# Issuing the stores of a two-layer transformer sandwich from ScalarE's DMA queue instead of SyncE's

## What is computed

```python
x = x + _layernorm(_L0_attn_ref(_layernorm(x), mask, weight, bias))
x = x + _layernorm(_L0_ffn_ref(_layernorm(x), W_up, gate_w, expert_bias, lora_A, lora_B))
```

## Time and profile before

| | us |
|---|---|
| median of 2 runs | 1674.51 |
| lowest, highest of them | 1667.52, 1681.50 |
| profiled execution | 1665.05 |
| its span, slowest cores (0 and 7) | 1663.5 |
| its span, fastest core (4) | 1653.5 |

### The profile page before, as it was taken

The page is one execution under the profiler, slowest core; times in us unless marked ns, Lnnn a source line. Parts: engine busy times, 40 slices in busy tenths (PEclk is TensorE's granted clock), DMA queues, the critical chain, the costliest instruction groups (busy, mean ns, idle before and its releaser), DMA issues.

```text
span 1663.5 us, 26761 instructions; the slowest of 8 cores (1653.5 to 1663.5 us)
## 1 busy us (share of the span) xinstructions
PE 1113.3 (67%) x9240; PEld 869.2 (52%) x9240; DVE 573.2 (34%) x805; ACT 393.0 (24%) x1249; POOL 44.6 (3%) x88
## 2 busy tenths in 40 slices
PE   0211369889898999988122132999999999999300
PEld 0100147667676777767011011777777777777200
DVE  1466553654656546444544434000000000001533
ACT  1422432212121222222232332222222222222100
POOL 1000000000000000000000000000000000000000
PEclk9999999999999999999555555999999999999755
DMA  8913235676867677641342762142342343241288
GB/s 194 337 58 102 51 102 133 172 183 173 202 160 196 163 188 198 163 83 52 119 185 101 210 195 101 27 77 52 71 83 52 55 77 74 52 77 27 107 332 319
DMA packets 40000, 220.47 MB, mean 133 GB/s; under 512 B 4850, under 2 KB 4866, under 8 KB 21442
## 3 DMA queue, kind: packets, MB, share of 16 engines
q0 software_dynamic: 11792, 84.46, 25.9%
q1 hardware_dynamic: 27938, 134.30, 23.0%
q10 hardware_dynamic: 144, 0.00, 0.0%
HBM read 252.86 MB, written 33.55 MB: 172 GB/s over the span
## 4 chain that ended last, share of the span: by engine, by line
PE 50%; DVE 20%; DMA 17%; issue 9%; ACT 2%; DVEq 1%; SPq 0%; ACTq 0%; POOL 0%; POOLq 0%
PE pm L375 42%; DMA mring<-mw 12%; PE pt L215 5%; DVE psj_i L304 3%; DVE wmb L347 2%; DMA fm<-xmid 2%; PE pm L389 2%; DVE xbst L271 1%; DVE sums_h L256 1%; DMA mo<-x 1%; DVE mo L539 1%; DVEq L680 1%; DVE cmp L563 1%; DVE fm L658 1%; ACT junk L525 1%
## 5 line engine op out<-in xcount | busy, mean ns | idle before, releaser
L375 PE MATMUL pm<-wmb,fm 128*128 128x256 bf16 x8192 | 952.4, 275 | 38.3 <-PE pt L583 0.2
L375 PEld LDWEIGHTS pm<-wmb,fm 128*128 128x128 bf16 x8192 | 791.3, 99 | 176.7 <-issue 79.9
L395 ACT ACTIVATE mo<-pm 128x256 bf16<-128x256 f32 x256 | 98.3, 384 | 780.2 <-PE pm L382 406.4
L304 DVE TENSOR_REDUCE psj_i<-mring 128x32 int32<-128x1024 int32 x128 | 156.1, 1220 | 217.4 <-DMA mring<-mw 211.0
L215 PE MATMUL pt<-identb,xbst 128*128 128x128 bf16 x288 | 51.4, 288 | 204.5 <-DVE xbst L271 170.8
L186 DVE TENSOR_REDUCE st_d<-acc_s 128x1 f32<-128x16 f32 x8 | 1.4, 170 | 489.5 <-ACT junk L403 488.8
L347 DVE TENSOR_TENSOR wmb<-wmb,bmpj 128x4096 bf16<-128x4096 bf16 x32 | 141.6, 4425 | 11.7 <-DMA wmb<-bw 8.5
L215 PEld LDWEIGHTS pt<-identb,xbst 128*128 128x128 bf16 x288 | 24.8, 115 | 231.1 <-issue 231.1
L215 PE MATMUL pt<-identb,mo 128*128 128x128 bf16 x224 | 39.7, 288 | 102.1 <-DVE mo L539 93.7
L403 ACT ACTIVATE junk<-pm 128x256 bf16<-128x256 f32 x256 | 98.3, 384 | 23.8 <-ACT mo L395 0.4
L220 ACT COPY fm<-pt 128x512 bf16<-128x512 bf16 x128 | 75.0, 586 | 115.1 <-PE pt L215 115.1
(11 more groups left out here) (116 smaller groups left out, 364.5 us busy)
## 6 DMA issues: line engine op xcount, KB each, us to landing
mring<-mw SPq DMA_DIRECT2D x128, 512.0 KB, 5.2
wmb<-bw POOLq DMA_DIRECT2D x32, 1024.0 KB, 9.8
wmb<-bu POOLq DMA_DIRECT2D x32, 1024.0 KB, 7.9
mo<-x POOLq DMA_DIRECT2D x12, 1024.0 KB, 25.9
xst<-x SPq DMA_DIRECT2D x10, 1024.0 KB, 8.4
xmid<-xst SPq DMA_DIRECT2D x10, 1024.0 KB, 4.6
fm<-xmid SPq DMA_DIRECT2D x8, 1024.0 KB, 8.2
y<-fm SPq DMA_DIRECT2D x8, 1024.0 KB, 4.5
```

The lines of the kernel that those rows point to most:

```text
L304: return e.tensor_reduce(out=psj_i32[:, (j % 2) * 256 + pc * 32:(j % 2) * 256 + (pc + 1) * 32], in_=mring[idx % 2][:, :].rearrange("p (g w ...
L375: return e.matmul(bank[0:128, 0:NS], fm[:, k * 1024 + i * 128:k * 1024 + i * 128 + 128], wmb[j % 2][:, k * NS:(k + 1) * NS], start=(k == 0 ...
L395: return e.activation(out=mo[:, i * 4096 + j * NS:i * 4096 + (j + 1) * NS], in_=bank[0:128, 0:NS], func=AF.Identity, accum_out=acc_s[:, i ...
```

## The change

The engine that issues two kinds of stores is ScalarE instead of SyncE: the 16 stores to `xmid` in the middle stage and the 16 stores to `y` in the tail. Waits, semaphores, sizes and slots are as before. All loads stay on SyncE.

```diff
@@ -519,7 +519,7 @@
                         scalar=c_one[:, 0:1], in1=ap_slot,
                         op0=ALU.mult, op1=ALU.add, accum_out=sums_h[:, sl:sl + 1])
                 trh[h] = E("vector", fr, waits=[td[h], t_tmp, t_const], inc="sV")
-                xm_tok[(i, h)] = E("sync", lambda e, i=i, h=h, ap_slot=slots[h][0]: e.dma_start(
+                xm_tok[(i, h)] = E("scalar", lambda e, i=i, h=h, ap_slot=slots[h][0]: e.dma_start(
                     out=d_xmid[i * 128:(i + 1) * 128, h * HALF:(h + 1) * HALF], in_=ap_slot),
                     waits=[trh[h]], inc=store_sem(), amt=16)
                 tq = E("scalar", lambda e, ap_slot=slots[h][0], sl=sl: e.activation(
@@ -658,7 +658,7 @@
                 tos[h] = E("vector", lambda e, i=i, h=h, ap_slot=slots[h][0]: e.tensor_add(
                     ap_slot, ap_slot, mo[:, i * 4096 + h * HALF:i * 4096 + (h + 1) * HALF]),
                     waits=[td[h], t_tmp], inc="sV")
-                y_tok[(i, h)] = E("sync", lambda e, i=i, h=h, ap_slot=slots[h][0]: e.dma_start(
+                y_tok[(i, h)] = E("scalar", lambda e, i=i, h=h, ap_slot=slots[h][0]: e.dma_start(
                     out=o_y[i * 128:(i + 1) * 128, h * HALF:(h + 1) * HALF], in_=ap_slot),
                     waits=[tos[h]], inc=store_sem(), amt=16)
```

## The result

| | before | after |
|---|---|---|
| median of the runs, us | 1673.64 (10 runs) | 1651.90 (11 runs) |
| lowest, us | 1667.27 | 1648.02 |
| profiled execution, us | 1665.05 | 1651.42 |
| span of its slowest core | 1663.5 (0 and 7) | 1649.9 (5) |

The changed kernel takes 0.987 of the time before (95% interval 0.984 to 0.990, over the runs in the undisturbed state): 1.3% or some 22 us less, under 2%. The forecast was 1637 with a range of 1624 to 1658. The sign and the mechanism hold. The sum of the forecast was 28.9 us less; the medians differ by 21.7 and the profiled executions by 13.6.

The account below looks back on a forecast made before the run. The prediction took SyncE's list order, which keeps the tail's loads behind stores, as the bound. From the profiled 1665.05 us, less 32.9 in the tail, plus 4.0 in the middle stage, it got 1636.2, said 1637, range 1624 to 1658.

Parts of the forecast that it names:

- What bounds the kernel now: Tail: list order on SyncE keeps loads behind stores, a serial round of about 13 us a chunk, eight rounds.
- Tail, instruction side: Tail: load 1 issued during matmuls, loads 2 to 5 at 1552.8, adds done early, DMA engines the next bound.
- Tail, the term of the rate: Tail: 29.4 MB at 385 GB/s take 76.3 us, gain 32.9 us; bounds 326 and 424 GB/s.
- Middle stage: Middle stage: stores ahead of squares on ScalarE make square 1 0.5 us late; cost 4.0 us over eight chunks, 2.6 to 6.6.
- Sum: Whole kernel: profiled execution 1665.05 less 32.9 in the tail plus 4.0 in the middle stage, 1636.2 us.
- the two queues share badly: Tail: turns between loads and stores keep 326 to 360 GB/s, gain 19 to 27, time 1642 to 1650 us; chance 0.20.
- The queues share well: Tail: engines carry 405 to 424 GB/s, gain 37 to 40 us, time 1629 to 1632; chance 0.20.
- The tail doesn't move: Tail: DMA engines already the bound, so reordering issues does nothing; time 1669 us; chance 0.06.
- the slower case: Middle stage: each store issue holds ScalarE until its transfer lands, costing 70 us, time 1702; chance 0.04.

Follow-up runs that it names:

- sp_order: Against the kernel before: all DMAs stay on SyncE, only its list's order in the tail changes, loads of chunks 0 to 5 first; ratio 0.988, tail 87.9 to 93.0 us.

## Why the prediction came out as it did

**What bounds the kernel now.** Right. The lists kept the loads back, and the waits of the earlier trace rows are gone. `sp_order` shows that a new order alone, in one queue, is enough.

**Tail, instruction side.** Right at each point: load 1 while TensorE works, loads 2 to 5 at the last matmul, a share near 1 to the end, last add 20 us ahead of the end, DMA the new bound.

**Tail, the term of the rate.** This is the term that was mis-sized. I took 385 GB/s, "between 375 and 424 and nearer the first", for a gain of 32.9 us. Measured on core 5: 29.4 MB in 89.0 - 1.5 us, 336 GB/s, a gain of 22 to 23. At the forecast's own lower bound of 326 the sum gave 19.1, so the size is one that the bounds held but the choice missed. I read the rate from stretches of 4 to 8 us of a tail in which the neighbour had gaps, and took it for what the core would get when neither has any. My ground for that, 424 and 420 on cores 7 and 6 in the same window, was weak on two counts: 4 us are too short to say what lasts, and windows count from each core's own first instruction, which no row shows to be the same moment. A longer row was there, 345 GB/s at a share of 1.00 over 10 us at the entry; it shows one core, and I used it only for a rival. The same trace has it for all: from 40 to 80 us the eight cores move 334 to 344 GB/s each at a share of 0.99 to 1.00. With 345 the sum reads 29.4 / 0.345 = 85.1, plus 1.5, end at 1639.4, gain 24.1, and 1665.05 - 24.1 + 4.0 = 1645. Most of the gain needs no higher rate at all: at the old mean of 326 it would be 19.1 by the forecast's own sum. It comes from the 15.8 us after the last matmul (1552.8 to 1568.6) in which the core moved only 61 GB/s and now streams.

The Trainium skill (HBM Reference, Specifications (TRN2)) gives about 358 GB/s for each core of a pair when both stream and more for a core alone. The runs agree with it in kind: 336 to 347 in the mix on eight cores, 427 to 428 alone. I had set it against the trace and held the trace to disagree; it was my reading of the trace that was wrong, not the rule.

**Middle stage.** The mechanism was right to the instruction: one issue shows ahead of square 0, and store 1 must wait for square 0 and then delays square 1. The size was 4.0 us, measured 5.6 (0.70 a chunk), within 2.6 to 6.6. What was missing is small waits. In chunk 1 square 1 starts 0.72 us behind its add's end, 0.58 more than before, near the 0.5 taken. But chunk 1, from which the price was read, is the cheapest: the waits at L169 grew by 0.56 us there, and by 0.95 or more in chunks 2 and 5, where square 0 too came some 0.3 us later behind its store.

**Sum.** 22 to 23 less 5.6 is 17; the profiled executions differ by 13.6, because the slowest core entered the middle stage 2.0 us later and lost 0.7 in the projection, and the runs' medians by 21.7. The difference between these is the spread of the runs. It also moves the forecast: 1637 starts from an execution of 1665.05, and the median before is 1673.64, 8.6 above it. The tail's rate (some 10), the middle stage (1.6) and the low start (8.6) add up to 20 us; the median missed 1637 by only 15. The other 5 us are the spread of the runs, which is luck.

**The rivals.** Of mine, "the two queues share badly" gives the right rate (326 to 360) and tail gain (19 to 27), a time that misses by 2 us (1642 to 1650), and the wrong cause: `sp_order` has one queue and the same rate, and the single core has two queues and 428. "The queues share well" is what one core alone does. "The tail doesn't move" was out, and with it the reading of the Trainium skill's rule on spreading DMAs over engines as one that forbids a gain (DMA: Bandwidth & Descriptors, Rules for kernel authors): no bandwidth was gained, only order. ScalarE was not held by its issues in the middle stage (0.33 us each), so the slower case had no ground.

## What to carry to other kernels

A DMA queue is a list: a load behind a store waits for whatever the store waits for, so order the issues by when they can go, on one queue or two. When a change is to fill the DMA engines of all cores, take its rate from a long stretch in which every core streams, not from a short full stretch between gaps: the share reads 1.0 in both. A store issued by a computing engine costs its issue and its waits where it stands; put it where that engine waits anyway.

## What I had not expected of the hardware

- DMA share 1.01 went with 258, 343 and 429 GB/s in the same mix of transfers, depending on what other cores did; a core that came into its tail later took more (374) than the one that was there before (258).
- The first L517 comes at 747 us on one core alone (both kernels, one execution each) and at 783 to 801 on the eight of the changed kernel: some 35 to 55 us of the entry and the first projection go with the other cores' presence. What in those stages it is I did not test.
- That start varies by 17 us or more among the cores of one execution (783.0 to 800.9; 773.9 to 799.6 with the y stores alone), which is most of what separates the slowest core from the others and hides stage gains of 5 us in the times.
